# Cross attention with key pieces and value pieces in two PSUM banks, taken a step later, and the weighing in one step

## What is computed

```python
q = layernorm(x) @ Wq + bq                # 16 batches x 64 queries, 16 heads of 16
k, v = split(context @ Wkv + bkv)         # 16 batches x 1024 keys
scores = einsum('bhid,bhjd->bhij', q, k) * hd ** -0.5   # + bias and mask of the keys
attn = softmax(scores, axis=-1)
x = x + einsum('bhij,bhjd->bhid', attn, v) @ Wout + bout
```

## Time and profile before

| What | Value |
|---|---|
| Median of 3 runs | 1519.82 us (1519.37 to 1521.12) |
| Profiled execution, its own time | 1515.53 us |
| Span of the profile (first to last instruction) | 1513.7 us |
| PE busy | 1316.4 us, 87% of the span |
| PEld, DVE, ACT, POOL busy | 70%, 68%, 46%, 42% |
| The two cross attentions, steady part (28 half batches each) | 400.7 us each |
| Mean granted TensorE clock | 0.924 of full speed; 1.00 in the steady parts |

### The profile page before, as it was taken

How to read it: one execution, slowest core, us unless ns; L and a number is a source line. 1 busy time by engine, 2 the same in 40 slices (tenths; PEclk the granted TensorE clock), 3 DMA queues, 4 the chain that set the end, 5 groups by cost and what they waited for, 6 DMA issues and landing times. The chain is left out here.

```text
span 1513.7 us, 34580 instructions
## 1 busy us (share of the span) xinstructions
PE 1316.4 (87%) x12182; PEld 1054.6 (70%) x12182; DVE 1036.2 (68%) x2121; ACT 696.2 (46%) x1246; POOL 640.1 (42%) x576
## 2 busy tenths in 40 slices
PE   3899999999999788479965999999999998766687
PEld 2788878878887566368853788788787886545454
DVE  5677777777777465454425677777777777565686
ACT  2466666666665211011223566666666666123111
POOL 4455545555554223043314455555555554335000
PEclk9999999999999885579987999999999999969699
DMA  5776676766764120625536766667676663101000
GB/s 186 189 192 168 163 182 169 166 178 169 170 164 113 43 46 3 207 82 170 173 124 202 190 166 169 176 173 172 169 180 170 160 164 85 32 1 59 1 15 15
DMA packets 108372, 202.64 MB, mean 134 GB/s; under 512 B 43645, under 2 KB 65182, under 8 KB 108032
## 3 DMA queue, kind: packets, MB, share of 16 engines
q1 hardware_dynamic: 106752, 197.64, 50.4%
q0 software_dynamic: 1536, 3.88, 0.9%
HBM read 90.42 MB, written 12.78 MB: 68 GB/s over the span
## 5 line engine op out<-in xcount | busy, mean ns | idle before, releaser
L632 POOL TENSOR_SCALAR cross_prob<-cross_prob,cross_inverse 128x1024 f32<-128x1024 f32 x256 | 287.7, 1124 | 431.3 <-DVE cross_inverse L466 430.9
L566 ACT ACTIVATE cross_prob<-cross_negated,cross_negmax 128x1024 f32<-128x1024 f32 x256 | 293.9, 1148 | 241.6 <-DVE cross_negmax L458 241.6
L458 DVE CUSTOM_DVE_ANT_0 cross_negated<-cross_scores,cross_bias 128x1024 f32<-128x1024 f32 x256 | 311.2, 1216 | 13.5 <-issue 5.7
L373 PE MATMUL cross_turn<-ident,cross_prob 128*128 128x128 f32 x2048 | 274.3, 275 | 10.5 <-POOL cross_prob L632 9.2
L373 PEld LDWEIGHTS cross_turn<-ident,cross_prob 128*128 128x128 f32 x2048 | 238.2, 141 | 55.6 <-POOL cross_prob L632 14.4
L441 DVE SCALAR_TENSOR_TENSOR cross_key_lo<-cross_proj,cross_bk,cross_key_hi 128x512 fp32r<-128x512 f32 x124 | 93.1, 751 | 145.4 <-ACT cross_key_hi L557 145.4
L474 DVE COPY cross_probT<-cross_turn 128x512 f32<-128x512 f32 x256 | 175.7, 686 | 6.5 <-PE cross_turn L373 4.5
L614 POOL TENSOR_TENSOR cross_ctx_lo<-cross_raw,cross_ctx_hi 128x512 fp32r<-128x512 f32 x128 | 165.9, 1300 | 14.9 <-ACT cross_ctx_hi L549 14.9
L360 PE MATMUL cross_scores<-cross_keys,cross_qbd 96*128 96x512 f32 x512 | 168.9, 411 | 3.5 <-DMA cross_keys<-cross_key_hi 3.5
L313 PE MATMUL cross_proj<-cross_wv_hi,cross_ctx_lo 128*128 128x256 f32 x496 | 151.9, 306 | 15.9 <-DVE cross_key_lo L441 15.9
L575 ACT COPY cross_probT<-cross_turn 128x512 f32<-128x512 f32 x256 | 147.5, 576 | 28.0 <-PE cross_turn L373 27.3
(11 more groups left out here) (236 smaller groups left out, 1980.5 us busy)
## 6 DMA issues: line engine op xcount, KB each, us to landing
cross_keys<-cross_key_hi SPq DMA_DIRECT2D x512, 128.0 KB, 3.4
cross_raw<-in_ctxT SPq DMA_DIRECT2D x32, 1024.0 KB, 6.1
cross_keys<-cross_key_lo SPq DMA_DIRECT2D x256, 128.0 KB, 2.7
cross_bias<-bias_rows SPq DMA_DIRECT2D x32, 512.0 KB, 4.8
up_sb<-in_moe_w SPq DMA_DIRECT2D x8, 1024.0 KB, 9.4
down_sb<-in_moe_w SPq DMA_DIRECT2D x8, 1024.0 KB, 11.5
cross_stacked_q<-q_rows SPq DMA_DIRECT2D x96, 64.0 KB, 2.1
q_rows<-cross_negated SPq DMA_DIRECT2D x8, 256.0 KB, 2.3
```

Source lines behind the costliest of these rows:

```text
L373: last = pe.transpose(ps_t[part][:, k * P:(k + 1) * P], prob[n % 2][:, kt * P:(kt + 1) * P], ident)
L458: dve.tensor_tensor_reduce(negated[n % 2][:, :], ps_s[n % 2][:, :], bias_sb[par][:, :], -1.0, 3.0e38, ALU.add, ALU.min, negmax[:, n % 2:n ...
L566: act.activation(prob[n % 2][:, :], negated[n % 2][:, :], ACT.Exp, bias=negmax[:, n % 2:n % 2 + 1], scale=-1.0, accum_out=total[:, n % 2:n ...
L632: pool.tensor_scalar(prob[n % 2][:, :], prob[n % 2][:, :], inverse[:, n % 2:n % 2 + 1], 1.0, ALU.mult, ALU.mult).then_inc(prob_ready, 1)
```

## The change

- Key pieces go through bank `ps_p` and value pieces through bank `ps_o`, which they share with the weighing (`key_bank`, `value_bank`). In batch 0 the banks alternate as before.
- A key piece waits for `key_lo_done` of the key piece before it, a value piece for `value_copied` of the value piece before it. Value pieces 0 and 2 wait also for `out_copied`, and each weighing waits for the value pieces that went through its bank (`value_copied`).
- A new function `taken_at` sets the steps in which pieces are taken out of PSUM. It is one step after the products. Both `round_key` and `rest_key` move to it.
- `copy_value` moves from VectorE to ScalarE. On ScalarE the taking stands first in a step, ahead of the turned copy and the exponential, and the special order of steps 3 and 7 (`ROUND_FIRST`) goes.
- `weigh` does both halves in steps 5 and 1, at the end of the step.
- On VectorE `copy_out` moves ahead of `maxima` in steps 6 and 2.

```diff
--- before.py
+++ after.py
@@ -35,7 +35,6 @@
 
 KEY_STEPS = (1, 3, 5, 7)
 SPLIT_STEPS = (1, 2, 5, 6)
-ROUND_FIRST = (3, 7)
 SPREAD_STEPS = (3, 5)
 VALUE_STEPS = (2, 4, 6)
 
@@ -211,9 +210,24 @@
             if n == 0 and not is_first(b):
                 value_(b, par, len(VALUE_STEPS))
 
-        def bank(b, piece):
+        def taken_at(b, par, n, key, value_):
+
+            if n - 1 in KEY_STEPS and not in_last(b, 1):
+                key(b + 1, 1 - par, KEY_STEPS.index(n - 1))
+            if n == 0 and not is_first(b):
+                key(b, par, len(KEY_STEPS) - 1)
+            if n - 1 in VALUE_STEPS and not in_last(b, 1):
+                value_(b + 1, 1 - par, VALUE_STEPS.index(n - 1))
+            if n == 1 and not is_first(b):
+                value_(b, par, len(VALUE_STEPS))
+
+        def key_bank(b, piece):
 
             return (ps_p, ps_o)[piece % 2 if is_first(b) else 0]
+
+        def value_bank(b, piece):
+
+            return (ps_p, ps_o)[piece % 2 if is_first(b) else 1]
 
         def is_first(b):
             return isinstance(b, int) and b == 0
@@ -321,13 +335,16 @@
                 g, c = piece // 2, piece % 2
                 if piece == 0:
                     pe.wait_ge(lo_done, 4 * b + 4)
-                if is_first(b) and piece >= 2:
-                    pe.wait_ge(key_lo_done, piece - 1)
-                if not is_first(b):
-                    pe.wait_ge(value_copied, 4 * b + piece)
+                if is_first(b):
+                    if piece >= 2:
+                        pe.wait_ge(key_lo_done, piece - 1)
+                else:
+                    pe.wait_ge(key_lo_done, 4 * b + piece)
+                if isinstance(b, int) and b == 1 and piece == 0:
+                    pe.wait_ge(value_copied, 3)
                 at, cols = slice(g * P, (g + 1) * P), slice(c * 512, (c + 1) * 512)
                 for k in range(G):
-                    last = three_passes(pe, bank(b, piece)[:, :], (wk_hi[:, k, at], wk_lo[:, k, at]),
+                    last = three_passes(pe, key_bank(b, piece)[:, :], (wk_hi[:, k, at], wk_lo[:, k, at]),
                                         (ctx_hi[par][:, k, cols], ctx_lo[par][:, k, cols]), k == 0, k == G - 1)
                 last.then_inc(key_ready, 1)
 
@@ -338,12 +355,16 @@
                     if piece >= 2:
                         pe.wait_ge(value_copied, piece - 1)
                 else:
-                    pe.wait_ge(key_lo_done, 4 * b + piece + 1)
+                    pe.wait_ge(value_copied, 4 * b + piece)
+                    if piece == 2:
+                        pe.wait_ge(out_copied, 2 * b - 1)
+                    if piece == 0 and not (isinstance(b, int) and b == 1):
+                        pe.wait_ge(out_copied, 2 * b - 2)
                 for j in range(2):
                     t = 2 * piece + j
                     at = slice(t * P, (t + 1) * P)
                     for k in range(G):
-                        last = three_passes(pe, bank(b, piece)[:, j * D:(j + 1) * D], (ctx_hi[par][:, k, at], ctx_lo[par][:, k, at]),
+                        last = three_passes(pe, value_bank(b, piece)[:, j * D:(j + 1) * D], (ctx_hi[par][:, k, at], ctx_lo[par][:, k, at]),
                                             (wv_hi[:, k, :], wv_lo[:, k, :]), k == 0, k == G - 1)
                 last.then_inc(value_ready, 1)
 
@@ -373,20 +394,23 @@
                         last = pe.transpose(ps_t[part][:, k * P:(k + 1) * P], prob[n % 2][:, kt * P:(kt + 1) * P], ident)
                     last.then_inc(turn_ready, 1)
 
-            def weigh(b, par, g, half_keys):
+            def weigh(b, par, g):
 
                 s = 8 * b + 4 * g + 3
-                if g == 0 and half_keys == 0:
-                    pe.wait_ge(value_copied, 4 * b + 4)
-                pe.wait_ge((turn_copied_a, turn_copied_v)[half_keys], s + 1)
-                if half_keys == 0 and not (is_first(b) and g == 0):
+                if g == 0:
+                    pe.wait_ge(value_copied, 4 * b + (4 if in_last(b, 1) else 6))
+                elif not in_last(b, 1):
+                    pe.wait_ge(value_copied, 4 * b + 8)
+                if not (is_first(b) and g == 0):
                     pe.wait_ge(out_copied, 2 * b + g)
-                for kt in range(4 * half_keys, 4 * half_keys + 4):
-                    for j in range(4):
-                        last = pe.matmul(ps_o[32 * j:32 * j + 32, 0:P],
-                                         value[par][:, kt, g * P + 32 * j:g * P + 32 * j + 32],
-                                         probT[:, j, kt, :], start=(kt == 0), stop=(kt == KT_TILES - 1))
-                last.then_inc((half_weighed, pv_done)[half_keys], 1)
+                for half_keys in range(2):
+                    pe.wait_ge((turn_copied_a, turn_copied_v)[half_keys], s + 1)
+                    for kt in range(4 * half_keys, 4 * half_keys + 4):
+                        for j in range(4):
+                            last = pe.matmul(ps_o[32 * j:32 * j + 32, 0:P],
+                                             value[par][:, kt, g * P + 32 * j:g * P + 32 * j + 32],
+                                             probT[:, j, kt, :], start=(kt == 0), stop=(kt == KT_TILES - 1))
+                    last.then_inc((half_weighed, pv_done)[half_keys], 1)
 
 
             for j in range(NT // 2):
@@ -417,20 +441,15 @@
                 for n in range(8):
                     scores(b, par, n)
                     two_before(turn, b, n)
-                    if n == 6:
-                        weigh(b, par, 0, 1)
-                    if n == 2 and not is_first(b):
-                        weigh(b - 1, 1 - par, 1, 1)
                     project_at(b, par, n, project_key, project_value)
                     if n == 5:
-                        weigh(b, par, 0, 0)
+                        weigh(b, par, 0)
                     if n == 1 and not is_first(b):
-                        weigh(b - 1, 1 - par, 1, 0)
+                        weigh(b - 1, 1 - par, 1)
             batches(pe, body)
             for n in (6, 7):
                 turn(B - 1, n)
-            for half_keys in range(2):
-                weigh(B - 1, 1, 1, half_keys)
+            weigh(B - 1, 1, 1)
 
         @block.vector
         def _(dve):
@@ -438,14 +457,9 @@
                 g, c = piece // 2, piece % 2
                 at = slice(c * 512, (c + 1) * 512)
                 dve.wait_ge(key_hi_done, 4 * b + piece + 1)
-                dve.scalar_tensor_tensor(out=key_lo[:, g, at], in0=bank(b, piece)[:, :], scalar=bk[:, g:g + 1],
+                dve.scalar_tensor_tensor(out=key_lo[:, g, at], in0=key_bank(b, piece)[:, :], scalar=bk[:, g:g + 1],
                                          in1=key_hi[:, g, at].bitcast(F32), op0=ALU.add, op1=ALU.subtract
                                          ).then_inc(key_lo_done, 1)
-
-            def copy_value(b, par, piece):
-                dve.wait_ge(value_ready, 4 * b + piece + 1)
-                dve.tensor_copy(value[par][:, 2 * piece:2 * piece + 2, :],
-                                bank(b, piece)[:, :].rearrange("p (j d) -> p j d", j=2)).then_inc(value_copied, 1)
 
             def maxima(b, par, n):
                 s = 8 * b + n
@@ -514,8 +528,6 @@
             dve.wait_ge(rows_loaded, 16 * (2 + len(rows)))
             for piece in range(4):
                 rest_key(0, 0, piece)
-            for piece in range(4):
-                copy_value(0, 0, piece)
             dve.wait_ge(q_stored, 32 * G * T // 512)
 
             def body(b, par):
@@ -524,13 +536,13 @@
                         invert(b, n - 1)
                     elif not is_first(b):
                         invert(b - 1, 7)
-                    maxima(b, par, n)
-                    two_before(copy_turn, b, n)
                     if n == 6:
                         copy_out(b, 0)
                     if n == 2 and not is_first(b):
                         copy_out(b - 1, 1)
-                    project_at(b, par, n, rest_key, copy_value)
+                    maxima(b, par, n)
+                    two_before(copy_turn, b, n)
+                    taken_at(b, par, n, rest_key, lambda b, par, piece: None)
             batches(dve, body)
             invert(B - 1, 7)
             for n in (6, 7):
@@ -554,8 +566,13 @@
                 if c == 0 and not is_first(b):
                     for n in range(4 * g, 4 * g + 4):
                         act.wait_ge(keys_loaded[n], 48 * b)
-                act.activation(key_hi[:, g, c * 512:(c + 1) * 512], bank(b, piece)[:, :], ACT.Identity,
+                act.activation(key_hi[:, g, c * 512:(c + 1) * 512], key_bank(b, piece)[:, :], ACT.Identity,
                                bias=bk[:, g:g + 1]).then_inc(key_hi_done, 1)
+
+            def copy_value(b, par, piece):
+                act.wait_ge(value_ready, 4 * b + piece + 1)
+                act.copy(value[par][:, 2 * piece:2 * piece + 2, :],
```

(11 more changed lines are left out.)

## The result

The changed kernel takes 1448.93 us (median of 4 runs, 1447.42 to 1451.18) against 1519.99 us. The ratio is 0.954, with a 95% interval of 0.952 to 0.956, so the kernel is 71 us or 4.6% faster. The forecast was 1455 us. Between the two profiled executions the difference is 67.1 us by the runs (1515.53 to 1448.41) and by the spans (1513.7 to 1446.6). The sum of the prediction was 64.6.

The account below looks back on a forecast made before the run. TensorE was taken to set the pace. Gains of 0.47 + 0.25 + 0.18 + 0.14 + 0.11 = 1.15 us a half batch gave 64.6 us over two cross attentions, so 1519.8 to 1455 us, range 1447 to 1492.

Parts of the forecast that it names:

- The sum: 28 half batches x 1.15 us, with small terms at start and end: 32.3 us per cross attention, 64.6 for two.
- What bounds the kernel: Steady part of a cross attention: TensorE sets the pace; its half batch goes from 14.31 to 13.16 us.
- part 1: Two banks and taking a step later: TensorE's stalls of 0.47 and 0.25 us ahead of value and key pieces go.
- the bound from the other side: Interval from transposes to a value piece: 0.79 us taken; with 0.97 twice the half batch is 13.52.
- rival B: Stalls shrink but move: 0.97 ahead of value pieces, 0.25 still ahead of the key piece; 1491 us; chance 0.19.
- D: Whole kernel: no measurable change, below 0.2% (3 us); chance 0.04.
- Part 2: Weighing in one step: 1.88 us instead of 2 x 1.01, and the 0.18 ahead of the second half goes.
- Part 3: Softmax loop and copies on the other engines: they stay hidden behind TensorE, with slacks of 0.3 to 0.7 us.
- the smallest slack: Key piece of step 5 starts at 9.68; VectorE makes the rest of the one before by 9.39: slack 0.3 us.
- The end: Batch 15, without projections: second weighing half and `copy_out` inside the softmax loop lose 0 to 3.5 us, taken as 1.
- Rival A: TensorE is as full as its busy share says: no more than 15 us come back, 1505 us; chance 0.06.
- Rival C: Serial chain over the half batch: with links of 3.6 us instead of 2.92, 11 us slower, 1531 us; chance 0.09.

## Why the prediction was right

*What bounds the kernel* was right. TensorE lost 1.20 us a half batch where the sum had 1.15, and 13.11 us came where 13.16 were laid out. The three stalls of part 1 went, and the taking of an interval of 0.79 ahead of a value piece, and not 0.97, was right (0.80 measured). That was the bound from the other side, and rival B's larger part. Its smaller part, the 0.25 ahead of the key piece, went too, so neither B nor D (no change) came about.

*Part 2* had 1.88 for the undivided weighing, and 1.89 came. The kernel before with this part alone (and `copy_out` ahead of `maxima`) gained 0.32 a half batch, the forecast term. The other 0.88 belong to the two banks, the later taking and ScalarE's copies together.

*Part 3* held in each check but for the wait of 0.5 laid out for the context, which came only twice in 320 us. The laid-out times and the measured ones are 0.88 and 0.90 for `maxima`, 0.3 and 0.43 for the smallest slack, 0.7 and 0.88 for ScalarE's turned copy, 0.7 and 0.66 for VectorE's, 6.5 to 6.6 and 6.54 for the issue of the context. The experiments show that these places decide. Taking the cover away at any one of them (the same step, VectorE's copy, `copy_out` behind `maxima`) cost 1.0 to 3.5 us a half batch. The doubled operations put the limits where the slacks were, at ScalarE only just and at VectorE clearly.

*The sum* was 64.6 us, and the profiled executions gave 67.1. The steady parts gave 67.1 instead of 64.4, 0.05 a half batch more. The small terms are less sure. The gain of 1.1 at the start of each cross attention came (1.15 and 1.3), but the first scores of the first came 0.8 later, a stretch where the prediction put ScalarE's four copies at nothing. TensorE waits there for the transfer of the keys, in both kernels (1.6 us now, 1.3 before). Why they came later is not shown. The end, costed at 1 us for each, was 0.1 and 1.4. The mechanism named for it, `copy_out` and the weighing inside the loop of batch 15, cost 1.1, but 1.0 came back just before, which the sum did not have, and most of the 1.4 is a lower clock in one weighing. That these terms and the unchanged parts add up to nothing is luck. The other 4 us between the medians come from the choice of executions: the profiled one of the kernel before lay 4.5 us below its median, the one after 0.5 below.

*Rival A* is refuted: busy time fell by 26 us in each steady part (393.35 to 367.20) with the same 3925 matmuls, so the busy time of before had held stalls. By the Trainium skill (Perfetto Trace Analysis, "Identifying the Most-Contended Engine") the share of the weight loads tells more. Here it went from 81% to 88% while the matmul share went from 98% to 100%, so its headroom of 19% was not all to be had either. *Rival C* did not occur in this kernel. The run with pieces taken in the same step shows that it is real, and that 14.3 us is where it lands.

## What to carry to other kernels

Compare the starts of like pairs of instructions (transposes to product, with and without a releaser), since behind a busy share of 98% lay a loss of 8% here, 0.88 us in waits for other engines and 0.32 in the second start of the weighing, of 14.31. When a result moves to another bank, another step or another engine, lay out the loop of the engines that follow, and check each place by its time and not by the engine's sum: two banks without the later taking gave nothing, and VectorE's copy in its spare time gave back 1.0 of the 1.2 us. Where a bank is shared, whoever frees it must stand first in its engine's order.

## What the runs showed that was not expected

A TensorE wait of 2.1 us in each half batch made the granted clock fall to 0.50 (1.2 GHz) for about 3 us behind it, which cost another 1.4 us. The waits of TensorE of up to 0.9 and 1.3 us in the runs with the weighing in two steps and with VectorE's value copy left the clock at 1.00 from 100 to 400 us. A lower clock also stretched the last weighing of a cross attention. In the traces of the kernel before, the changed kernel (twice) and the version with the old order in the last batch, four of the eight took 1.95 or 1.96 us and the other four 2.81 to 3.16. Both kinds occur with both kernels, and what decides between them stays open.
